# Expert lookup on one core: exponentials moved from ScalarE to GpSimd, products one chunk ahead, the ends of the next layer collected behind its loop

## The reference, cut to what matters

```python
# L2F: h (128 wide) and the top 8 of each of 8 heads come first
de, ue = down_embed[indices], up_embed[indices]       # 2048 x 128 and 2048 x 256
z = einsum('btd,bthkd->bthk', h, de)
z = silu(z * softmax(sc))                             # sc: 8 scores of each head
out = einsum('bthk,bthkd->btd', z, ue);  x = x + out
# L3X: k', v from the context, q' from layernorm(x)
q, k = relu(q @ Wqf.T), relu(k @ Wkf.T) * mask
kv, k_sum = sum_s k'_s v_s, sum_s k'_s                # over 2048 context tokens
out = (q' kv) / (q' k_sum + 1e-8);  x = x + out @ Wo.T + bo
```

## Time and profile before

| | us |
|---|---|
| median of 3 runs | 1339.32 (1335.14 to 1339.72) |
| profiled execution, its own time | 1336.76 |
| span of its profile | 1334.9 |
| the two layers, from the first gather to the last addition to x | 866.7 to 1161.1 |
| steps of L3X, from the first key product to the last summary | 867.7 to 1123.3 |
| last weighted sum of the lookup ends | 1143.1 |

### The profile page before, as it was taken

How to read it: one execution, slowest core, us unless ns; L and a number is a source line. 1 busy time by engine, 2 the same in 40 slices (tenths; PEclk the granted TensorE clock), 3 DMA queues, 4 the chain that set the end, 5 groups by cost and what they waited for, 6 DMA issues and landing times.

```text
span 1334.9 us, 22850 instructions
## 1 busy us (share of the span) xinstructions
PE 1140.2 (85%) x9353; PEld 817.2 (61%) x9353; DVE 696.4 (52%) x1532; ACT 482.1 (36%) x1069; POOL 165.4 (12%) x168
## 2 busy tenths in 40 slices
PE   6987889977877999999999977856986976777998
PEld 5866556656654555555556655735764755676886
DVE  3543456763326777655666253462626647374332
ACT  1101146762312355655566833222332321121322
POOL 0004000000001000000000000073635462000000
PEclk9998999998987999999999999977978957786999
DMA  9021200003003000000000020152524241003552
GB/s 365 1 95 48 111 1 1 2 2 154 0 16 135 1 2 2 1 2 1 2 2 2 2 77 1 54 145 63 152 70 123 78 113 48 14 0 158 198 204 81
DMA packets 16182, 84.38 MB, mean 63 GB/s; under 512 B 3152, under 2 KB 3664, under 8 KB 12368
## 3 DMA queue, kind: packets, MB, share of 16 engines
q1 hardware_dynamic: 7888, 57.75, 11.3%
q0 software_dynamic: 8192, 25.17, 6.7%
HBM read 82.65 MB, written 0.26 MB: 62 GB/s over the span
## 4 chain that ended last, share of the span: by engine, by line
PE 74%; DVE 12%; issue 5%; ACT 4%; another core or an unknown queue 3%; POOL 1%; DMA 1%; POOLq 0%; SPq 0%; DVEq 0%; ACTq 0%
PE L2X_bank_ring L1762 6%; PE L2X_bank_ring L1778 6%; PE L2X_bank_read L1792 5%; PE L2X_bank_ring L1701 4%; PE L2F_bank_sim L2389 3%; PE L1X_banks_scores L910 3%; PE L2X_bank_ring L1710 2%; PE L1X_bank_proj L887 2%; PE L0X_bank_k L457 2%; PE L2F_bank_keys L2347 2%; PE L3F_bank_y L3327 2%; PE L0X_bank_moments L468 2%; PE L2F_banks_pair L2364 2%; PE L3F_bank_gathered L3276 2%
## 5 line engine op out<-in xcount | busy, mean ns | idle before, releaser
L2059 DVE TENSOR_REDUCE L2X_max_parts<-L2X_bank_ring 128x1 f32<-128x512 f32 x256 | 158.3, 684 | 85.7 <-PE L2X_bank_ring L1762 85.7
L1970 ACT ACTIVATE L2X_context_exp<-L2X_bank_ring 128x384 f32<-128x384 f32 (+1 forms) x384 | 144.5, 465 | 62.1 <-PE L2X_bank_ring L1778 59.5
L2477 POOL DMA_INDIRECT L2F_rows<-in_L2F_embed_dram,L2F_expert x128 | 132.3, 1033 | 107.8 <-DVE x L2698 50.4
L1762 PE MATMUL L2X_bank_ring<-L2X_context_kT,L2X_q_masked 32*128 32x512 f32 x512 | 96.9, 630 | 0.0
L1016 ACT ACTIVATE L1X_probs<-L1X_clipped,L1X_drop,L1X_keep 128x1024 f32<-128x1024 f32 x64 | 77.9, 1240 | 32.1 <-DVE L1X_clipped L1075 24.9
L2389 PEld LDWEIGHTS L2F_bank_sim<-L3X_v_ones,L3X_k_features 128*128 128x128 f32 x512 | 72.1, 211 | 26.0 <-issue 24.2
L1075 DVE TENSOR_SCALAR L1X_clipped<-L1X_banks_scores 128x1024 f32<-128x1024 f32 x64 | 75.4, 1220 | 24.1 <-PE L1X_banks_scores L910 22.3
L2389 PE MATMUL L2F_bank_sim<-L3X_v_ones,L3X_k_features 128*128 128x34 f32 x512 | 69.2, 285 | 20.0 <-issue 19.8
L1778 PE MATMUL L2X_bank_ring<-L2X_q_and_max,L2X_context_kT 32*128 32x384 f32 (+1 forms) x768 | 86.0, 497 | 0.0
L1792 PEld LDWEIGHTS L2X_bank_read<-L2X_context_exp,L2X_context_v_ones 128*32 128x32 f32 x2048 | 50.2, 109 | 43.8 <-issue 33.4
L1792 PE MATMUL L2X_bank_read<-L2X_context_exp,L2X_context_v_ones 128*32 128x128 f32 x2048 | 75.8, 277 | 1.1 <-ACT L2X_context_exp L1970 0.8
(11 more groups left out here) (618 smaller groups left out, 2075.6 us busy)
## 6 DMA issues: line engine op xcount, KB each, us to landing
L3F_expert_weights<-in_L3F_experts_dram SPq DMA_DIRECT2D x16, 1280.0 KB, 5.6
L1A_groups<-in_L1A_groups_dram SPq DMA_DIRECT2D x3, 1536.0 KB, 9.6
ctxT<-in_ctxT_dram SPq DMA_DIRECT2D x8, 512.0 KB, 10.5
L0X_tokens<-in_L0X_tokens_dram SPq DMA_DIRECT2D x8, 512.0 KB, 15.0
slot<-in_L1A_dram SPq DMA_DIRECT2D x1, 3584.0 KB, 11.4
slot<-in_L0F_dram SPq DMA_DIRECT2D x1, 3072.0 KB, 11.0
slot<-in_L2A_dram SPq DMA_DIRECT2D x1, 3072.0 KB, 10.8
slot<-in_L2F_dram SPq DMA_DIRECT2D x1, 2476.5 KB, 9.7
```

The lines of the kernel that those rows point to most:

```text
L1762: nc.tensor.matmul(bank[:, :], qm[32 * g:32 * g + 32, b, c, j, :], cT[32 * g:32 * g + 32, s % 3, blk * 512:(blk + 1) * 512], start=True, s ...
L1970: nc.scalar.activation(ex[:, n % NE, g, 0:width(s)], bank_of(s_e, done(n) + g + 1)[:, 0:width(s)], ACT.Exp, scale=SCALE).then_inc(s_e, 1)
L2059: nc.vector.tensor_reduce(parts[:, j, g, blk:blk + 1], bank_of(s_ft, n)[:, :], AX, ALU.max).then_inc(s_ft, 1)
L2477: pool.indirect_dma_start(out=rows[:, r, k, :], out_offset=None, in_=env.dram["L2F_embed"], in_offset=bass.IndirectOffsetOnAxis(idx[:, b, ...
```

## The change

It has five parts.

1. The exponentials go to POOL as powers: the constant tile `one_by_e` (exp(-1) in 32 columns) raised to z, or to a softmax argument whose sign is turned. Only the first softmax (batch 0) stays on ACT. POOL takes them in the middle of a chunk, after its fourth gather: `exp_z(n - 2)` in chunk n, and ahead of it the softmax of the heads in chunks 8 and 12. Those of the last three pieces follow the last gather.
2. DVE runs `products(m)` ahead of `weighted_sum(m - 1)`; z, exp(-z) and the weights get three places instead of two. The later two `choose` stand ahead of pieces 6 and 9.
3. The ring uses three places for chunks 0 to 8 and four from chunk 9 on.
4. `FRONT` is 2 instead of 3. `exp_after` is gone.
5. In the loop of L3X only five items of `finish(0, n)` are left. The other two and all of `finish(1, n)` are mixed behind the loop, behind 10 idle products instead of 24, in other PSUM banks, and without the wait for the last z. On DVE `divided(0)`, `kv_blocks(1)` and `add_out(0)` come behind the last weighted sum.

```diff
-    ring = [0, 1, 2, 0, 1, 2, 3] + [n % 4 for n in range(len(chunks) - 7)]
+    ring = [n % 3 for n in range(9)] + [(n + 3) % 4 for n in range(len(chunks) - 9)]
...
-    FRONT, FINISH = 3, 25
-    exp_after = {1: 0, 4: 1, 6: 2, 8: 3, 13: 4, 16: 5, 17: 6, 21: 7, 23: 8, 25: 9, 26: 10, 27: 11, 29: 12, 31: 13}
+    FRONT, FINISH = 2, 25
...
-            finish(0, n - FINISH, bank_k, bank_k, (bank_k, bank_k), bank_k)
+            if n - FINISH < 5:
+                finish(0, n - FINISH, bank_k, bank_k, (bank_k, bank_k), bank_k)
         summary(len(steps) - 1)
         pe.wait_ge(s_fc, len(steps))
-        pe.wait_ge(s_vc, len(steps))
-        pe.wait_ge(s_z, len(pieces))
-        idle_products(M, bank_v, 24)
-        for n in range(7):
-            finish(1, n, bank_x, bank_p0, (bank_p1, bank_h), bank_p0)
-            if n in (0, 4, 5):
-                idle_products(M, bank_v, 4)
+        idle_products(M, bank_v, 10)
+        finish(1, 0, bank_k, bank_k, None, bank_k)
+        finish(1, 1, bank_k, bank_k, None, bank_k)
+        finish(0, 5, bank_kv[0], None, None, None)
...
+        def exp_z(m):
+            _, lo, hi = pieces[m]
+            pool.wait_ge(s_z, m + 1)
+            nc.gpsimd.tensor_tensor(ze[:, m % 3, lo:hi], per_e[:, lo:hi], zz[:, m % 3, lo:hi], ALU.pow).then_inc(s_ze, 1)
+
+        def exp_soft(part):
+            b, lo, hi = parts[part]
+            pool.wait_ge(s_sh, part + 1)
+            many = soft[:, b, lo:hi, :].rearrange("p h k -> p (h k)")
+            nc.gpsimd.tensor_tensor(many, per_e[:, 0:(hi - lo) * TOP], many, ALU.pow).then_inc(s_se, 1)
...
+                if k == TOP // 2 - 1:
+                    if chunks[n] in [p[0:2] for p in parts[2:]]:
+                        exp_soft([p[0:2] for p in parts].index(chunks[n]))
+                    if n == 10:
+                        rstd3[0].gpsimd(pool)
+                    if n >= 2:
+                        exp_z(n - 2)
+        for m in range(len(chunks) - 2, len(pieces)):
+            exp_z(m)
...
-            products(m)
-            if m == 13:
-                divided(0)
-            weighted_sum(m)
-            if m == 14:
-                add_out(0, bank_k)
-                kv_blocks(1)
+            if m < len(pieces):
+                products(m)
+            if m:
+                weighted_sum(m - 1)
```

More of the change, by code:

```diff
@@ L2540, in copy_keys @@
                 nc.scalar.activation(kT[:, n % 2, c, :], bank_k[:, :], ACT.Identity, bias=w3("bk")[:, c:c + 1]).then_inc(s_kc, 1)
[L2542 to L2549, removed]
         def finish(b, n, bank_t, bank_q, bank_f):
@@ L2583, in _ @@
                 act.wait_ge(s_sh, 2)
[L2584 to L2590, removed]
+                nc.scalar.activation(soft[:, 0, :, :], soft[:, 0, :, :], ACT.Exp, scale=-1.0).then_inc(s_se, 1)
             if n % 4 == 0 and n // 4 + 1 < len(steps) // 4:
@@ L2593, in _ @@
             front(n - FRONT)
-            finish(0, n - FINISH, bank_k, bank_k, (bank_k, bank_k))
[L2595 to L2598, removed]
+            if n - FINISH < 5:
+                finish(0, n - FINISH, bank_k, bank_k, (bank_k, bank_k))
+        finish(1, 0, bank_k, None, None)
+        finish(1, 1, None, bank_k, None)
+        finish(0, 5, bank_kv[0], None, None)
+        finish(1, 2, None, None, (bank_p0, bank_p1))
+        finish(1, 3, None, None, (bank_p0, bank_p1))
+        finish(1, 5, bank_k, None, None)
     @block.vector
@@ L2683, in products @@
             chain(nc.vector.tensor_tensor(down, down, hn[:, b, :].unsqueeze(1).to_broadcast([P, hi - lo, P]), ALU.mult))
-            chain(nc.vector.tensor_reduce(zz[:, m % 2, lo:hi], down, AX, ALU.add))
-            nc.vector.tensor_tensor(zz[:, m % 2, lo:hi], zz[:, m % 2, lo:hi], soft[:, b, h, lo:hi], ALU.mult).then_inc(s_z, 1)
+            chain(nc.vector.tensor_reduce(zz[:, m % 3, lo:hi], down, AX, ALU.add))
+            nc.vector.tensor_tensor(zz[:, m % 3, lo:hi], zz[:, m % 3, lo:hi], soft[:, b, h, lo:hi], ALU.mult).then_inc(s_z, 1)
         def weighted_sum(m):
@@ L2752, in _ @@
         normalise(0, 0, RH, 1)
-        for m in range(len(pieces)):
-            if m == 4:
+        for m in range(len(pieces) + 1):
+            if m == 6:
                 natural_h(1, bank_e1)
                 choose(*parts[2], 5)
-            if m == 7:
+            if m == 9:
                 choose(*parts[3], 5)
@@ L2760, in _ @@
                 normalise(*parts[2], 2)
-                norm3(0)
             if m == 12:
@@ L2764, in _ @@
                 kv_blocks(0)
-            products(m)
-            if m == 13:
-                divided(0)
-            weighted_sum(m)
-            if m == 14:
-                add_out(0, bank_k)
-                kv_blocks(1)
+            if m < len(pieces):
+                products(m)
+            if m:
+                weighted_sum(m - 1)
+            if m == 8:
+                moments3(0)
+            if m == 9:
+                norm3(0)
+        moments3(1)
         norm3(1)
+        divided(0)
+        kv_blocks(1)
+        add_out(0, bank_kv[0])
         divided(1)
-        add_out(1, bank_p0)
+        add_out(1, bank_k)
     M.stack.close()
```

37 lines of the change are left out of this document (24 added, 13 removed).

## The result

The changed kernel took 1284.19 us (median of 4, 1281.47 to 1287.00) beside 1339.52 us for the kernel before on the same chip: ratio 0.9582, 95% interval 0.9535 to 0.9630, a gain of 55.3 us. The forecast was 1316 us with a range of 1284 to 1345 and a gain of 20.7 us; the direction was right, the size was not, and the time is that of rival B (1287 us). Some executions of one kernel run at a lower granted clock and take over 1.5% longer; the medians given for before in group 3, e5 and e9 include one or two of these, the ratios leave them out.

A forecast was written before the change was run, and what follows sets the result against it. The lookup set the end, with PE held up beside gathers; after the change PE's loop counts, ending at 1123 us. Plus a 17.4 us tail: x at 1140.4 against 1161.1, gain 20.7, forecast 1316 us, range 1284 to 1345.

The forecast's parts named there:

- rival B: PE held up much less, 7.5 matmuls a us, done by 1020; lookup sets the end: 1287 us, gain 50; chance 0.20.
- The step that failed: PE's L3X loop: 835 matmuls at 3.9 a us beside gathers, 260 after; loop ends at 1123 us, as now.
- The path: Something that goes with gathering holds up PE, through PE ACT, and through ACT the exponentials; DVE waited 78.9 us for them.
- the burst from 928 us on: Gathers at 928 to 979 us: had short breaks yet lost speed at its end; cited against rival B.
- The pace of the gathers: On POOL: 1.31 us per gather; last gather ends at about 1080 us instead of 1110, lookup at about 1094.
- The wait for chunk 8: POOL's chunk 8 needs the third `choose`, which needs PE's sixth front item, now in step 7; 7 us allowed.
- Powers of 8 columns: New powers on POOL: 1.6 us each, bounds 1.0 to 2.0; 5.0 us for 32 columns, bounds 1.0 to 8.1.
- The wait for z that was to cost nothing: POOL waits in chunk n for z of chunk n - 2; no cost unless DVE stands in certain other work.
- The waits for exponentials: DVE's waits for exponentials were to shrink from 78.9 us to under 20.
- The tail: Behind PE's loop: idle products 3 us, chain to x 12.7, two items 1.7; 17.4 us instead of 37.8.
- C: PE held up more beside one 214 us gathering stretch, 2.2 matmuls a us: 41 us later, 1378 us; chance 0.22.
- D: POOL's powers cost more, lookup stays later; counts from 3.5 us each, gain gone at 5 us, some 1337; chance 0.08.

The follow-up runs named there:

- group 3: e9 to e12, run beside the kernel before on the same chip; before took 1342.86 us.
- e5: The kernel before, unchanged, as a control: 1341.42 us.
- e9: The changed kernel with exponentials and both softmaxes of batch 1 back on ACT, bound to PE's steps, no pauses on POOL: 1333.22 us, ratio 0.9907 to before.
- e10: e9's kernel plus an idle 8-column power on POOL after the fourth gather of chunks 2 to 15: 1277.95 us, ratio 0.9518 to before.
- e11: The kernel before plus 14 idle 8-column powers on POOL between gathers, exponentials still on ACT: 1299.37 us, ratio 0.966 to before.
- e6: The changed kernel, unchanged, run again beside before: 1283.96 us, ratio 0.9564.
- Groups 1, 4 and 5: Runs beside the kernel before, which took 1281.03, 1280.89 and 1280.43 us there.
- e3: Same kernel as e9 (changed kernel, exponentials back on ACT, no pauses), run in another group: 1244.30 us, ratio 0.9706 to before.
- groups 2 and 3: Runs beside the kernel before, which took 1340.26 and 1342.86 us there.
- e7: The changed kernel with its two 32-column softmaxes on ACT instead of POOL, z powers staying on POOL: 1274.57 us, ratio 0.9521 to before.
- e12: The changed kernel, unchanged, run again beside before: 1281.34 us, ratio 0.9560.
- e4: Same kernel as e10 (changed kernel, exponentials on ACT, idle powers as pauses), run in another group: 1265.51 us, ratio 0.9899 to before.
- e1: Same kernel as e11 (before plus 14 idle powers between gathers), run in another group: 1281.01 us, ratio 1.0012 to before.
- e8: The changed kernel plus an idle 8-column power on POOL in the middle of chunks 0 and 1: 1283.99 us.

## Why the prediction was wrong

**The step that failed** is "While gathers run, 866 to 1080 = 214 us, I let it do 3.9 a us as before: 835", with its reason, "the same 128 gathers stand beside the same products, only with fewer long pauses". It priced the hold-up by the number of gathers. The runs show that the spacing of the gathers counts: beside the same 128 gathers and the same products PE did 4.8 matmuls a us instead of 3.6 (e10 against e9), and 4.7 instead of 4.1 (e11 against e5), as soon as a power stood between each eight of them. The kernel before had three long pauses; here fourteen of about 2 us did it. The sum had the powers as a price on POOL alone, 14 x 1.9 us, and not as relief for PE. PE's loop ended at 1086.7 instead of 1123 us.

**The path was told too simply** as well: "So something that goes with gathering holds up PE, and through PE ACT". ACT is held up by itself. In the kernel before, ACT has to copy the features of PE's third product next. It stands idle from 892.9 to 912.1 us, though that product had ended at 888.3:

```profile
887.17 1.13 PE L2364 MATMUL L2F_banks_pair<-slot,L3X_kT 64*128 64x256 f32 x8
```

```profile
912.10 1.02 ACT L2575 ACTIVATE L3X_k_features<-L2F_banks_pair 128x1024 f32<-128x1024 f32 x1 [19.21 <-remote]
```

PE was held up by itself too: in the same stretch matmuls of one summary (L2389), which wait for nothing between them, start up to 2.4 us after each other's end.

The facts were on the table. The prediction says that "the first windows after a pause run better than the last ones before it", and rival B says "gathers break every 12.4 us for 1.9 us of a power, and before the hold-up showed only some 15 to 20 us into a burst". The prediction set that argument aside for one counterexample, the burst from 928 us on. Its short breaks, 4.2 and 2.0 us, lay early. Its loss of speed came where gathers followed on each other from 956 to 977 us; the window of the kernel before, columns as in the earlier trace rows:

```profile
963.00:979.00 16.00, 9.54 (x34) 7.34 (x33) 4.29 (x11) 2.19 (x4) 10.80 (x11) 0.56 0.52 147
```

**Rival B** was given 0.20. Its bound was right: the lookup sets the end, at 1094 + 17 = 1111 us (measured 1095.5 + 15.3 = 1110.7), and 1287 us. Its rate was not: 7.5 a us was assumed, 4.9 came, and PE's loop was done at 1086.7, not 1020. Since only the later of the two streams counts, that error cost nothing; that its total came out is in part luck. PE's rate scatters: e6 did 4.4 a us (937 in 212 us), its loop ended at 1096.6, 3.9 us behind the last weighted sum, and the time was the same.

The Trainium skill, "SBUF — State Buffer", section "SBUF: two separate sides", says that engine ports and DMA ports are disjoint and that a DMA cannot slow an engine. Groups 1, 4 and 5 fit it (in e3 PE did 1059 matmuls in 176 us beside gathers, 6.0 a us), groups 2 and 3 do not, as far as PE's rate goes. By which way gathers reach the engines no trace shows, so these groups don't prove the rule wrong.

**The pace of the gathers** was right: the last one ends at 1081.8 us (said: about 1080), the last weighted sum at 1095.5 (about 1094). The wait for chunk 8 took 8.0 us, allowed 7. Powers of 8 columns took 1.74 us in the mean (said 1.6), those of 32 took 5.46 (5.0), each inside its bounds. The wait for z that was to cost nothing cost 3.7 us in chunk 2.

**The waits for exponentials** were to fall under 20 us and fell to 36.3. Two of them, 10.3 and 7.8 us, stand behind the powers of the softmaxes: 5.46 us, and the power of z behind that. The prediction had counted these powers on POOL's side and not for DVE. e7 took them away: these waits fell from 37.5 us (e6) to 25.6, and the time by some 9.

**The tail** was mis-sized little: 24.0 us behind the last summary where 15 to 19 was said, because 9 of these are the wait for the lookup; in e6, where PE was last, 13.4 us against 17.4. (The sum takes 3.5 us of idle products as 3.)

**Rivals C and D**: the rate rose (4.8 against 3.9 where gathers run), so C fell. D needed 3.5 us for each power of z, and they took 1.74; but as in D, the last weighted sum ended after PE's loop, because the loop was early.

**How the 55 us divide.** By the ratios of group 3, with hold-ups, pauses alone gave some 46 us (e11), all the rest of the change without pauses 12 (e9), both together 65 (e10) or, with the powers on POOL, 59 (e12). The gains don't add up singly: the rest gave 36.7 us where nothing was held up (e3). With the same pauses, exponentials on ACT, bound to steps that fit the new order, did as well as powers on POOL. So taking the exponentials from ACT gave nothing that these runs show; a power that stands on POOL served as the pause.

**A version that beats both kernels.** e7 did, in its group: 1274.57 us against 1283.96 and 1340.26. e10 took 1277.95 against 1281.34 for the changed kernel in group 3, but the two sets of four times overlap. Without hold-ups e3 is the best, 1244.30, and it is nearly the worst with them, 1333.22.

## What to carry to other kernels

When gathers stand in a long row and the other engines show waits that no instruction explains, try another POOL instruction between them, and count the unbroken row, not the gathers. Price an added instruction on an engine also for what its pause lets others do. Before you take a wait put to "issue" or "remote" at its word, look at the timelines of the engines that it could be for. And run the kernel before beside each variant, on more than one occasion: the pauses that cost 21 us on one occasion (e4 to e3) saved some 52 us on another (e10 to e9).

## What the runs showed of the hardware that was not expected

**Hold-ups beside gathers come and go with the occasion.** One chip gave the kernel before 1342.86 us in one group and 1280.43 in another, with all runs of a group on one side (1333.76 to 1355.33, and 1275.81 to 1283.43). In the groups without, no wait of PE (weight loads aside), ACT or DVE between 860 and 1110 us is put to "issue" or "remote"; the end of the program behind x took the same time in both (173.8 us in e1 and in the first profile of before), so only the stage of gathers differs. What sets the condition is open.

**Where there are hold-ups, records of events are missing.** Each gather adds 16 to a semaphore, 2048 landings in all. The traces of the ten profiles without hold-ups hold 2065 to 2078 recorded landings between 860 and 1125 us (some are of other transfers), the ten with hold-ups 529 (e9) to 964 (e8). For that reason the view of the transfers gives a time to landing (3.1 us) for e1 and none for e11, the same kernel (first e1, then e11):

```profile
L2F_rows<-in_L2F_embed_dram,L2F_expert POOLq DMA_INDIRECT x125, 3.1
```

```profile
L2F_rows<-in_L2F_embed_dram,L2F_expert POOLq DMA_INDIRECT x112
```

Two things follow. In these profiles a wait put to "issue" or "remote" can be one whose record is lost, like the 11.05 us above. And it may be that the recording of events itself holds the engines up and that a pause lets it catch up: the two profiles with the most records among the ten, e8 and e11, are also those with the shortest waits of PE put to "issue" (5.2 and 4.0 us from 860 to 1110 us, 12.9 to 38.4 in the others). It is not shown. Every execution on record has a span and a granted clock of its own, so none is known to have run unrecorded, and no run tells this rival from one in which gathers hold up engines that are not watched.

**In e9 PE paid twice for its waits**, once in the waits and once in the granted clock behind them: 0.59 from 960 to 1020 us in e9, 1.00 in e3.

**Powers and weighted sums ran beside each other at full length.** DVE's and POOL's timelines of the changed kernel:

```profile
1016.35 4.16 DVE L2712 SCALAR_TENSOR_TENSOR x<-L2F_rows,L2F_expert_weight,x 128x256 f32<-128x256 f32 x8
```

```profile
1018.93 1.68 POOL L2472 TENSOR_TENSOR L2F_z_exp<-L2F_one_by_e,L2F_z 128x8 f32<-128x8 f32 x1
```

Eight instructions that each read two tiles of SBUF took 4.16 us, as elsewhere, while a power with two tiles of its own ran from 1018.93 to 1020.61, beside the last of them, in 1.68 us. Three of the eight lie wholly inside the power and took 485 ns each, as long as those ahead of it. The Trainium skill, "SBUF — State Buffer", section "SBUF: two separate sides", says that such a pair locks each other out for the whole length of an instruction. This trace disagrees.
